# A fused attention and mixture-of-experts layer: the router's sigmoid from silu and a division, with its steps moved

## What is computed

```
xn = layernorm(x)
hid = relu(xn @ nm_w1 + b1);  m = hid @ nm_w2 + b2
attn = softmax(window of 65 keys of (m Wq)(m Wk)^T / sqrt(128)) (m Wv)
gates = xn @ gate_w^T;  scores = sigmoid(gates)            # 16 experts
top 8 of scores + expert_bias; their scores / their sum * 2.826 = combine
y = sum_e combine_e * (silu(xn Wg_e) * (xn Wu_e)) Wd_e  + the same for one shared expert
out = x + attn + y
```

## Time and profile before

| | us |
|---|---|
| three runs of the kernel before | 683.79, 684.12, 684.91 |
| median | 684.12 |
| the profiled execution | 684.41 |
| its span, first to last instruction | 682.6 |
| PE busy in it | 673.7 (99%) |
| DVE busy | 615.5 (90%) |
| ACT, POOL busy | 448.1, 431.3 |
| one group, from the fourth on | 41.12 to 41.19 |

### The profile page before, as it was taken

The page is one execution under the profiler, slowest core; times in us unless marked ns, Lnnn a source line. Parts: engine busy times, 40 slices in busy tenths (PEclk is TensorE's granted clock), DMA queues, the critical chain, the costliest instruction groups (busy, mean ns, idle before and its releaser), DMA issues.

```text
span 682.6 us, 10378 instructions
## 1 busy us (share of the span) xinstructions
PE 673.7 (99%) x3080; PEld 543.5 (80%) x3080; DVE 615.5 (90%) x1687; ACT 448.1 (66%) x918; POOL 431.3 (63%) x386
## 2 busy tenths in 40 slices
PE   8999999999999999999999999999999999999997
PEld 6877788788888878788887888888888787888875
DVE  6999999999999999999999999999899999898875
ACT  5875666657676575766766676576766757576573
POOL 4785665666657656676566657656676566656553
PEclk9999999999999999999999999999999999999999
DMA  8607155261633717155271642717245171532600
GB/s 266 238 2 290 51 174 199 85 243 57 231 130 102 270 34 279 61 164 210 61 265 48 219 153 97 270 38 264 79 145 227 42 279 39 198 144 62 233 1 16
DMA packets 38040, 101.80 MB, mean 149 GB/s; under 512 B 8672, under 2 KB 18144, under 8 KB 29920
## 3 DMA queue, kind: packets, MB, share of 16 engines
q1 hardware_dynamic: 37984, 101.14, 41.7%
HBM read 92.42 MB, written 8.70 MB: 148 GB/s over the span
## 4 chain that ended last, share of the span: by engine, by line
PE 87%; DVE 5%; DMA 3%; ACT 2%; issue 1%; SPq 1%; DVEq 0%; ACTq 0%
PE ps_u L511 25%; PE ps_y L521 25%; PE ps_g L501 25%; PE bank L432 3%; DVE ps_u L1193 1%; PE bank L481 1%; PE ps_y L491 1%; PE bank L472 1%; PE bank L465 1%; PE bank L443 1%; DMA exp_raw<-wexp 1%; DVE h_lo L1199 1%; DMA h_dram<-exp_raw 1%; PE bank L454 1%; PE bank L483 1%
## 5 line engine op out<-in xcount | busy, mean ns | idle before, releaser
L1325 POOL TENSOR_TENSOR silu_c<-silu,comb_b 128x512 f32<-128x512 f32 x252 | 326.9, 1300 | 229.2 <-ACT silu L766 229.2
L774 ACT ACTIVATE h_hi<-ps_u 128x512 fp32r<-128x512 f32 x272 | 163.2, 600 | 217.6 <-DVE ps_u L1193 217.5
L1199 DVE TENSOR_TENSOR h_lo<-ps_u,h_hi 128x512 fp32r<-128x512 f32 x272 | 185.5, 682 | 26.8 <-ACT h_hi L774 23.7
L1193 DVE TENSOR_TENSOR ps_u<-silu_c,ps_u 128x512 f32<-128x512 f32 x256 | 176.7, 690 | 16.9 <-PE ps_u L511 11.7
L766 ACT ACTIVATE silu<-ps_g 128x512 f32<-128x512 f32 x272 | 161.8, 595 | 0.2
L511 PE MATMUL ps_u<-xn_hi,exp_w_hi 128*128 128x512 f32 x272 | 112.4, 413 | 1.3 <-DVE h_lo L1199 1.2
L521 PE MATMUL ps_y<-h_hi,exp_w_hi 128*128 128x512 f32 x272 | 109.0, 401 | 0.9 <-DVE h_lo L1199 0.6
L501 PE MATMUL ps_g<-xn_hi,exp_w_hi 128*128 128x512 f32 x272 | 108.2, 398 | 1.3 <-ACT silu L766 1.3
L521 PE MATMUL ps_y<-h_lo,exp_w_hi 128*128 128x512 f32 x272 | 107.4, 395 | 0.0
L521 PE MATMUL ps_y<-h_hi,exp_w_lo 128*128 128x512 f32 x272 | 107.3, 395 | 0.0
L511 PE MATMUL ps_u<-xn_hi,exp_w_lo 128*128 128x512 f32 x272 | 107.3, 395 | 0.0
(11 more groups left out here) (160 smaller groups left out, 960.6 us busy)
## 6 DMA issues: line engine op xcount, KB each, us to landing
comb_b<-c_dram SPq DMA_DIRECT2D x63, 1024.0 KB, 7.2
mom_b<-st_dram SPq DMA_DIRECT2D x13, 512.0 KB, 3.8
xres<-x_t SPq DMA_DIRECT2D x16, 256.0 KB, 2.6
out_t<-xres SPq DMA_DIRECT2D x16, 256.0 KB, 2.0
xin<-x SPq DMA_DIRECT2D x15, 256.0 KB, 3.0
h_dram<-exp_raw SPq DMA_DIRECT2D x60, 64.0 KB
exp_raw<-h_dram SPq DMA_DIRECT2D x15, 256.0 KB, 3.1
xn<-x_t SPq DMA_DIRECT2D x13, 256.0 KB, 3.3
```

The source lines that it names most:

```text
L774: A(h_t[hbuf(par, s)][0][:], ps_u[(par + s) % 2][:], ACT.Copy).then_inc(s_h_hi, 1)
L1193: V.tensor_tensor(ps_u[i][:], src[:], ps_u[i][:], ALU.mult).then_inc(s_h, 1)
L1199: V.tensor_tensor(t[1][:], ps_u[(par + s) % 2][:], t[0][:].bitcast(F32), ALU.subtract)\
L1325: G.tensor_tensor(silu_c[i][:], silu[i][:], comb_b[:, s1 - 1, :], ALU.mult).then_inc(s_silu_c, 1)
```

## The change

- **Router arithmetic.** sigmoid(x) = silu(x) / x. The exp on ACT becomes a silu (`gate_sig`), the add of 1 goes, the reciprocal is now of the sum itself (`route_inverse`) and needs no result of ACT, and a product joins them. Since x may be 0, three small operations ahead of it (`off_zero`) add 2e-15 where x is smaller than 1e-15: on POOL in step 5 (8 in group 0), and on DVE in the prologue.
- **Steps moved, groups 1 and up:** PE's gate product 4 to 5, second scores 5 to 6; ACT's router function 5 to 7; DVE's `h_prod` ahead of the second `row_max` in step 6, the first `normalise_probs` behind `h_lo` in step 6, reciprocal in 7, `route_scores` 7 and `route_max` 8 to 9, `route_match` 9 to 10, `route_sum` 10 to 11, `prob_lo` 9 and 10 to 10 and 11, `route_weights` 11 to 12, ahead of `hid_blocks`.
- **Prologue and group 0:** ACT's first table is that of silu (`warm`), so that no switch lies before the first silu; the side products go to `bank[2]` in place of `ps_u[1]`, which lets the second `up_proj` go ahead of the wait for the combine weights; three splits of expert weights go behind the first silus; DVE's `score_weights` goes from step 3 to 2; group 0's router steps move, and `hid_blocks` goes from 12 to 13.

```diff
-                pe.wait_ge(S["gate_s"], g + 1)
+                pe.wait_ge(S["gate_1"], g + 1)
...
-                side = ps_u[1]
+                pe.wait_ge(s_attw, 1)
+                side = bank[2]
...
-                if s == when(g, 4, 7) and more:
+                if s == when(g, 5, 7) and more:
-                if s == when(g, 5, 7):
+                if s == when(g, 6, 7):
...
+                if first(g) and s == 1:
+                    up_proj(g, par, s)
                 att_early(g, par, s)
...
-            def gate_exp(g):
-                act.wait_ge(S["gate_s"], g + 1)
-                A(flat(gate_e), flat(gate_s), ACT.Exp, scale=-1.0).then_inc(S["gate_e"], 1)
+            def gate_sig(g):
+                if first(g):
+                    act.wait_ge(S["gate_first"], 1)
+                else:
+                    act.wait_ge(S["gate_s"], g)
+                    act.wait_ge(S["score"], g)
+                A(flat(gate_e), flat(gate_s), ACT.Silu).then_inc(S["gate_e"], 1)
...
+                act.wait_ge(s_spin, 1)
+                A(warm[:], spin_in[:, 0:1].bitcast(F32), ACT.Silu)
...
                 expw_hi(1)
                 expw_hi(2)
-                gate_exp(0)
-                expw_hi(3)
-                expw_hi(4)
+                gate_sig(0)
...
                 if s == when(g, 5, 8):
-                    if more:
-                        gate_exp(g + 1)
                     prob_exp(g, 0)
+                if s == when(g, 7, 9) and more:
+                    gate_sig(g + 1)
...
-                V.tensor_scalar(gate_1[:], gate_e[:], 1.0, None, ALU.add).then_inc(S["gate_1"], 1)
-                dve.wait_ge(S["gate_1"], g + 1)
-                V.reciprocal(score[:], gate_1[:]).then_inc(S["score"], 1)
+                dve.wait_ge(S["inv_gate"], g + 1)
+                V.scalar_tensor_tensor(out=score[:], in0=gate_e[:], scalar=1.0, in1=inv_gate[:],
+                                       op0=ALU.mult, op1=ALU.mult).then_inc(S["score"], 1)
...
+            def off_zero(g):
+                pool.wait_ge(S["gate_1"], g + 1)
+                G.tensor_tensor(near0[:], gate_1[:], gate_1[:], ALU.mult).then_inc(S["near0"], 1)
+                pool.wait_ge(S["near0"], g)
+                G.tensor_scalar(near0[:], near0[:], TINY * TINY, 2.0 * TINY, ALU.is_lt, ALU.mult)                    .then_inc(S["moved0"], 1)
+                pool.wait_ge(S["moved0"], g)
+                pool.wait_ge(S["gate_e"], g)
+                pool.wait_ge(S["score"], g)
+                G.tensor_tensor(gate_s[:], near0[:], gate_1[:], ALU.add).then_inc(S["gate_s"], 1)
...
-                if s == when(g, 9, 12):
+                if s == when(g, 10, 12):
                     prob_lo(g, 0)
...
-                if s == when(g, 11, 12) and more:
-                    route_weights(g + 1, 1 - par)
...
                 if s == 12 and more:
+                    route_weights(g + 1, 1 - par)
+                if s == when(g, 12, 13) and more:
                     hid_blocks(g + 1)
...
+                if some:
+                    h_prod(*before(g, par, s))
                 if s == when(g, 6, 9):
                     row_max(g, 1)
-                if first(g) and s == 3:
-                    score_weights()
-                if some:
-                    h_prod(*before(g, par, s))
                 att(g, par, s)
...
+                if s == 6 and not first(g):
+                    normalise_probs(g, 0)
```

More of the change, by code:

```diff
@@ L31 @@
 TAKEN = -3e38
+TINY = 1e-15
 RUNS = 8
@@ L229, in layer @@
         names = """bn aggr var_eps rstd mean centred0 centred1 xn xn_tp xn_hi xn_lo gate_mm gate_h gate_s gate_e
-            hid_b gate_1 score select top8 rest weight wsum winv comb comb_t
+            hid_b gate_1 near_first gate_first near0 moved0 inv_gate score select top8 rest weight wsum winv comb comb_t
             hid_mm hid hid_hi hid_lo q_mm q_hi q_lo hid_tp hn_hi hn_lo key_term
@@ L676, in slot @@
                 att_late(g, par, s)
-                up_proj(g, par, s)
+                if not first(g) or s != 1:
+                    up_proj(g, par, s)
                 if first(g) and s == 3:
@@ L854, in slot @@
                     act.wait_ge(s_side_mm, 1)
-                    A(chain[:, 1, :], ps_u[1][:, M_B:M_B + P], ACT.Copy).then_inc(s_side, 1)
+                    A(chain[:, 1, :], bank[2][:, M_B:M_B + P], ACT.Copy).then_inc(s_side, 1)
                 else:
@@ L922, in gate_sum, with off_zero, route_inverse @@
                 dve.wait_ge(S["gate_h"], g + 1)
-                V.tensor_reduce(gate_s[:], gate_h[:].rearrange("p a (n e) -> p a e n", n=2), AX.X, ALU.add)\
-                    .then_inc(S["gate_s"], 1)
+                if g > 1:
+                    dve.wait_ge(S["gate_s"], g - 1)
+                V.tensor_reduce(gate_1[:], gate_h[:].rearrange("p a (n e) -> p a e n", n=2), AX.X, ALU.add)\
+                    .then_inc(S["gate_1"], 1)
+            def off_zero():
+                dve.wait_ge(S["gate_1"], 1)
+                V.tensor_tensor(near0[:], gate_1[:], gate_1[:], ALU.mult).then_inc(S["near_first"], 1)
+                dve.wait_ge(S["near_first"], 1)
+                V.tensor_scalar(near0[:], near0[:], TINY * TINY, 2.0 * TINY, ALU.is_lt, ALU.mult)\
+                    .then_inc(S["near_first"], 1)
+                dve.wait_ge(S["near_first"], 2)
+                V.tensor_tensor(gate_s[:], near0[:], gate_1[:], ALU.add).then_inc(S["gate_first"], 1)
+            def route_inverse(g):
+                if first(g):
+                    dve.wait_ge(S["gate_first"], 1)
+                else:
+                    dve.wait_ge(S["gate_s"], g)
+                V.reciprocal(inv_gate[:], gate_s[:]).then_inc(S["inv_gate"], 1)
             def route_scores(g):
@@ L1052, in prologue @@
                 gate_sum(0)
+                off_zero()
+                route_inverse(0)
                 route_scores(0)
@@ L1170, in fresh_att @@
                     hid_lo(0)
+                    score_weights()
                     variance(1)
@@ L1214, in slot @@
                     h_lo(*before(g, par, s))
+                if s == 6 and not first(g):
+                    normalise_probs(g, 0)
                 if first(g) and s == 1:
                     moments(1, 1)
-                if first(g) and s == 9:
-                    route_scores(1)
             def finish():
@@ L1279, in prologue @@
                 pool.wait_ge(S["xn"], 1)
-                for s in range(0, 3):
+                for s in range(0, 2):
                     expw_lo(s)
+                expw_lo(2)
                 pool.wait_ge(S["comb"], 1)
@@ L1337, in slot @@
                         centre(g + 2, 1)
+                if s == when(g, 5, 8) and not last(g):
+                    off_zero(g + 1)
                 if s == when(g, 2, 5):
```

29 lines of the change are left out of this document (17 added, 12 removed).

## The result

The changed kernel takes **691.56 us** (median of 6 runs, 690.18 to 692.58), 1.0108 of the kernel before (95% interval 1.0095 to 1.0121): 7.5 us slower. Forecast were 692.4 us and a range of 682 to 698. The total was right, and in part by luck: two of its terms were wrong in opposite directions, and what follows is mostly about them. ("Changed kernel" is the one with the whole change, "kernel before" the one without.)

A forecast was written before the change was run, and what follows sets the result against it. TensorE was taken as the bound, busy 673.7 of 682.6 us. Groups 2 to 14 +9.0, group 15 +0.5, group 1 -0.7, prologue and group 0 -0.5: +8.3 on 684.12 gives 692.4 us, range 689 to 697 (8 in 10: 682.0 to 698.0).

The forecast's parts named there:

- So the reload moves with `comb_t`: SP's queue: reload waits behind `comb_t`'s store, spread and hidden-layer stores, so `route_weights` in step 12 delays it 1.75 us.
- X: Start of `hid_n_hi`, counted behind its group's start: 1.23 us before, forecast 2.98; the waits are counted from it.
- Upper end of the shift: Delay of `comb_t` and the reload: at most 2.00 us, at least 1.6 if DVE reaches step 12 sooner; 1.75 taken.
- The third wait: PE's `up_proj` of step 4 waits for `h_lo` of step 2, behind `xn_lo`: 0.27 us a group.
- The first wait: PE's `up_proj` of step 2, ready at X + 2.56: 0.16 us and a toll, 0.26 a group.
- the second: PE's `down` of step 3 waits for `finish_group`, ending at X + 4.31, 0.05 for hand-over: 0.40 us a group.
- The gains of 0.24 a group: Groups 1 and up: -0.10 for `xn_lo`, about 0.06 for the silu wait, 0.08 for `h_lo` of step 8.
- tolls: PE's exposed part of a weight load that comes late but inside the matmul ahead: about 0.1 us each.
- The maxima leave step 8: DVE, step 8: without the maxima `h_lo` comes 0.3 us sooner, so one toll of 0.08 us goes.
- New operations: DVE's new product and POOL's `off_zero`: covered, nothing taken, 0 to 0.2 us a group kept for DVE stretched beside POOL.
- Prologue and group 0: Table load leaving the first silu credited 0.2 us, less router work in steps 9 to 13: together -0.5 (-1.9 to +0.5).
- the reload is absorbed: Rival: ACT's slack and DVE's free time, or closer transfers, soak up the shift; only gains stay, 679.5 us; chance 0.17.

The follow-up runs named there:

- e2: Kernel before with only `route_weights` moved from step 11 to 12, ahead of `hid_blocks`: 696.36 us, ratio 1.0175.
- e6: Kernel before with `route_weights` moved from step 11 to 12 and the hidden rows' stores issued ahead of the first spread: 683.06 us, ratio 0.9984.
- e1: Changed kernel with the combine weights (`route_weights`) made in step 11 again in groups 1 and up: 697.93 us, ratio 1.0198.
- e3: Changed kernel with SP's queue turned, the four hidden-layer stores issued ahead of the first spread of the combine weights: 688.86 us, ratio 1.0071.
- e11: Changed kernel with hidden-layer stores ahead of the first spread and GpSimd's `off_zero` left out in groups 1 to 15: 688.16 us, ratio 1.0055.
- e10: Changed kernel with hidden-layer stores ahead of the first spread and the silu-times-inverse product on one of four tiles in groups 1 to 15: 687.51 us.
- e7: Kernel before with the changed kernel's prologue alone, without the shift off zero; later groups' router as before: 684.27 us, ratio 1.0004.

## Why the prediction came out as it did, point by point

**The mechanism held.** "So the reload moves with `comb_t`": yes, and e2 with e6 shows it to be the whole price of the moved weights in the kernel before. The two waits were forecast from group 1 as X + 2.56 and X + 4.36. In group 2 of the changed kernel (start 105.22, X 3.31, so `hid_n_hi` at 108.53) and in the one from 478.44 (`hid_n_hi` at 480.93) the weight loads say:

```profile
111.09 0.19 PEld L515 LDWEIGHTS ps_u<-xn_hi,exp_w_hi 128*128 128x128 f32 x1 [0.78 <-DVE h_lo L1241]
...
112.89 0.19 PEld L525 LDWEIGHTS ps_y<-h_hi,exp_w_hi 128*128 128x128 f32 x1 [0.56 <-DVE xres L1112]
...
485.29 0.19 PEld L525 LDWEIGHTS ps_y<-h_hi,exp_w_hi 128*128 128x128 f32 x1 [0.38 <-DVE xres L1112]
```

108.53 + 2.56 = 111.09; 108.53 + 4.36 = 112.89; 480.93 + 4.36 = 485.29.

**"Upper end of the shift 2.00, lower end 1.6; I take 1.75": the step was wrong twice.** The store moved by 2.05 (12.91 to 10.86), a hair beyond the upper end: VectorE doesn't reach step 12 sooner, since the product and the choice took the time that the weights had given up. But X moved by 1.41 only (1.27 to 2.68), because the reload followed 10.30 behind the store and not 10.97. That "nothing there overtakes" is right, that the transfers keep their spacing is not. The reload follows the spread's issue 9.1 us behind in the kernel before, 8.3 in the changed one, 8.5 in e1 and 8.6 in e2; e2 comes to 11.10 all the same because there the spread is issued 2.5 us behind the store, and 1.9 to 2.0 in the others. What shortens the part behind the spread I haven't settled; e1 has it with an early store, so it isn't the lateness. With X 2.98 forecast and 2.68 measured, this term was too large by 0.30 a group. The price of a given X was nearly right in sum: the changed kernel's group with X 3.02 took 41.77, 0.61 above the kernel before, where 0.69 was forecast for 2.98; those with X 2.28 and 2.31 took 41.05. The parts of that price were not right:

**The third wait, `up_proj` of step 4, never came, and I can say why.** The prediction gave `xn_lo` 1.36 us, "never less in 13 groups". It is 0.73 in all 13 now. Before, it began just behind GpSimd's `mask_k` and had to let it finish; in the changed kernel it begins first, and GpSimd waits. Timelines of VectorE and GpSimd before, then after:

```profile
439.50 1.37 DVE L912 TENSOR_TENSOR xn_lo<-xn,xn_hi 128x512 fp32r<-128x512 f32 x1
```

```profile
439.44 0.86 POOL L1304 TENSOR_TENSOR mask_k<-mask,low_k 128x320 f32<-128x320 f32 x1
```

```profile
486.34 0.74 DVE L930 TENSOR_TENSOR xn_lo<-xn,xn_hi 128x512 fp32r<-128x512 f32 x1
```

```profile
486.49 1.33 POOL L1357 TENSOR_TENSOR mask_k<-mask,low_k 128x320 f32<-128x320 f32 x1
```

The medians have changed sides: `xn_lo` 1359 to 731 ns, `mask_k` 872 to 1330. (In e2 `xn_lo` is 728, in e3, with the reload early, 1373.) VectorE wins back 0.6 us exactly when it is late, so 0.27 of the forecast 0.93 was not to be had. The first wait (0.26) appeared only where X was above some 2.8; at the usual 2.5 the loads of step 2 are in time. What stays at X 2.5 is the second, with a loss of some 0.2 at 485 us, where 0.40 was forecast for X 2.98.

**The gains of 0.24 a group:** the tolls of `xn_lo` (13 times) and of the silu went, 0.16. "The maxima leave step 8, so one toll of 0.08 goes" failed: a group of e3 is 0.17 us ahead of one of the kernel before at `up_proj` of step 9, and 0.11 behind it at step 13. In between stand late loads of `up_proj` in steps 10 and 11 (0.45 and 0.25 us in the mean; the kernel before has one of 0.26 in step 10). Two held-up instructions of VectorE share in them. One is the product: in group 14 it takes 0.75 and not 0.90, and the group is 0.16 shorter (41.12). The other is `xn_lo`, earlier in the same group: where it takes 0.74 the group takes 40.99. In the one group where both came out short (e11's group 14, `xn_lo` 0.69, product 0.74) it is 40.84, which is the forecast gain and a little more. So the gains were there, and VectorE meeting GpSimd took them back. In all, groups 2 to 14 cost 3.6 us where 9.0 were forecast.

**"New operations: nothing, 0 to 0.2 a group"** was too low in its basis. I set the Trainium skill's rule aside (SBUF — State Buffer, "SBUF: two separate sides") because L930 had one input in SBUF. The section names VectorE's operations in a two-port mode beside those with two SBUF inputs, and I had read over the first half. It says that of a VectorE and a GpSimd instruction the one that starts first keeps the shared port to its end. The traces agree in every case looked at: VectorE's stretched instructions of 64 columns end 0.05 to 0.09 us behind GpSimd's (12.16 and 12.10 in the prologue, 44.43 and 44.35, 45.39 and 45.31, 337.85 and 337.77), and `xn_lo` with 512 columns 0.55 behind. The wait itself doesn't depend on the size (e10), and the roles swap with the order of the starts (`xn_lo` and `mask_k`). Two of those held have only one input in SBUF: the shift's second instruction (0.89 us) and the old add of 1 where it took 729 ns. The old add of 1, mostly 189 ns, lay where GpSimd was idle (before, at 449.40, GpSimd rested from 446.52 to 450.81). The new product lies in step 9: it began at 294.49, GpSimd's `silu_c` at 294.03, and they ended at 295.40 and 295.31.

**Prologue and group 0, -0.5 forecast, +2.70 measured: the term that failed.** Of the prologue (0.61) the bound of +0.5 was nearly the truth: "+0.4 us on `comb`", covered by the second `up_proj`, was 0.96, since the shift's second instruction waited for GpSimd (0.89 us, above) and `comb` came at 15.55 though the gate product had begun 0.57 earlier. Where it didn't wait (e3, e11) `comb` was 0.26 later, counted from the gate product, and PE still waited 0.36 for it. The question "what is late next" was the right one and the answer wrong by some half a microsecond. For steps 9 to 13 I counted what VectorE loses and not what it gets at that very place: product, choice and maxima ahead of `h_lo` in step 10, two of them held up by GpSimd. That cost 1.63 us by step 11, and with the 0.6 of steps 13 to 15, whose cause is open, it made 2.09 in place of a gain of 0.3 to 0.9. That there would have been room by the sizes alone (0.23 + 0.23) is my count and no run's.

**So the errors of -5.2 in groups 1 to 15 and +3.2 ahead of them made one of -2.0 in the profiled execution, and of -0.8 in the median.** That is luck: with either error alone the total would have been off by 3 to 5 us. The late reload was the right mechanism, but the largest term of the sum, 13 times 0.93 or 12 us, stands against 2.7 us that turning the queue gives back. The rival "the reload is absorbed" was refuted, X 2.7 with 14 waits for `xres`. The price of a table load, 1.28 us by the row, was not put to the test: taken out of the prologue it gave 0.4 us in the profile of e7, and less than that by the means over all profiles. The Trainium skill (ScalarE: Activation LUTs, "What ACT_TABLE_LOAD costs") has 2.66 us; no row here shows more than the 1.28.

## What to carry to other kernels

When a producer moves back, look at what is queued behind it and ask whether the queue's order can give the time back: here one turned pair of DMA issues made a cost of 12 us vanish, and was worth 0.18% to the kernel that nobody had moved anything in. Price a small VectorE instruction by where it starts against GpSimd's work, not by its size or by its median elsewhere. And before a stage is credited with a gain because work leaves it, list what comes in at the same place.

## What the chip showed that I had not expected

- A later transfer can make a group faster: with X 2.26 one group of e3 took 40.99 us, its neighbours with X near 1.1 took 41.27 to 41.32, because `xn_lo` then started ahead of GpSimd's `mask_k` and didn't wait for it.
- A VectorE instruction on 16 columns takes 849 ns beside GpSimd's `silu_c` of 1.29 us, one on 64 columns 900 ns, and 225 ns where GpSimd is idle. The wait goes either way: GpSimd's 0.86 us became 1.33 when VectorE had started first.
- Four stores of 64 KB behind a spread of 1024 KB held a reload back until 8.3 us after the spread's issue (469.50 to 477.76); ahead of it, the reload was issued 5.1 us behind the first of them (467.22 to 472.33), but then took 6.1 us to land beside the spreads, where it had taken 3.1.
- One line of VectorE's schedule, moved by one step, cost 12.2 us (1.0175) by way of that queue, more than the whole change (7.5).
